# Norm, turn and split of the MLP's first chunk made inside the output projection

## What is computed

```python
x = x + attn_a(layernorm(x), Wq, bq, Wk, bk, Wv, bv, Wo, bo)   # softmax(q k^T) v, then @ Wo.T + bo
x = x + ffn(layernorm(x), gate_w, ..., down_s)                 # (silu(x @ gate) * (x @ up)) @ down
x = x + attn_b(layernorm(x), w_gate, w_up, w_down)             # silu, the smaller half set to 0, * up, @ down
x = x + ffn(layernorm(x), gate_w, ..., down_s)                 # the same weights again

def layernorm(x, eps=1e-05):
    m, v = mean(x), var(x)                                     # over the 512 features
    return (x - m) / sqrt(v + eps)
```

## Time and profile before

| | us |
|---|---|
| median of 3 runs | 1960.66 |
| lowest and highest run | 1959.5 and 1961.62 |
| the profiled execution, its own time | 1961.3 |
| span of that execution (first to last instruction) | 1959.5 |
| TensorE busy in it | 1834.5 |
| VectorE busy in it | 1426.4 |
| ScalarE busy in it | 1030.8 |
| GpSimd busy in it | 754.4 |

### The profile page before, as it was taken

How to read it: one execution, slowest core, us unless ns; L and a number is a source line. 1 busy time by engine, 2 the same in 40 slices (tenths; PEclk the granted TensorE clock), 3 DMA queues, 4 the chain that set the end, 5 groups by cost and what they waited for, 6 DMA issues and landing times.

```text
span 1959.5 us, 39587 instructions
## 1 busy us (share of the span) xinstructions
PE 1834.5 (94%) x14968; PEld 1124.2 (57%) x14968; DVE 1426.4 (73%) x2798; ACT 1030.8 (53%) x1888; POOL 754.4 (39%) x922
## 2 busy tenths in 40 slices
PE   7998888999899798998999999999999999999989
PEld 3443333333333475775776667665766766757756
DVE  6567788788882313996978888887888888878821
ACT  4334677777774122753654545635645636546411
POOL 4685656566772111224116125132142242232331
PEclk9998999899999898999999999999999999999989
DMA  7864554455433604005232213225143042161010
GB/s 245 243 196 141 146 143 123 123 144 176 137 113 122 219 1 127 12 12 151 75 126 42 91 64 104 85 62 158 41 130 88 12 152 63 33 183 54 12 41 11
DMA packets 217133, 205.70 MB, mean 105 GB/s; under 512 B 136400, under 2 KB 173264, under 8 KB 216992
## 3 DMA queue, kind: packets, MB, share of 16 engines
q1 hardware_dynamic: 210992, 187.77, 33.5%
q0 software_dynamic: 4272, 12.91, 2.0%
q10 hardware_dynamic: 1728, 3.15, 0.4%
HBM read 147.39 MB, written 33.62 MB: 92 GB/s over the span
## 4 chain that ended last, share of the span: by engine, by line
PE 55%; DVE 4%; POOL 3%; DMA 1%; issue 1%; ACT 1%; SPq 0%; DVEq 0%; ACTq 0%
PE acc L1517 14%; PE ga L1507 13%; PE ub L1507 13%; PE ga L1535 5%; PE ub L1535 5%; PE acc L1550 5%; DVE junk L1651 1%; DMA pp<-ax 1%; POOL lohi L1453 1%; POOL pp L1463 1%; POOL d_xs L1308 1%; POOL rstd_f L1271 1%; POOL ax L1469 1%; DVE kept L1701 0%; DVE junk L1686 0%
## 5 line engine op out<-in xcount | busy, mean ns | idle before, releaser
L1453 POOL TENSOR_TENSOR lohi<-h,lohi 128x256 f16<-128x256 f32 x224 | 171.8, 767 | 729.8 <-ACT lohi L1598 729.5
L1587 ACT ACTIVATE kept<-ax,T 128x1376 f16<-128x1376 f32 x248 | 356.9, 1439 | 149.7 <-DVE T L1659 146.1
L1651 DVE TENSOR_SCALAR_CACHE_REDUCE junk<-ax,T 128x1376 f16<-128x1376 f32 x248 | 405.9, 1637 | 0.9
L1067 ACT ACTIVATE pr<-s 128x512 f32<-128x512 f32 (+2 forms) x640 | 320.2, 553 | 97.5 <-PE s L956 76.9
L649 DVE TENSOR_REDUCE mx<-s 128x2 f32<-128x1024 f32 (+2 forms) x300 | 319.8, 1113 | 65.2 <-PE s L628 33.8
L1507 PE MATMUL ga<-xT_f,w_gate 128*128 128x256 f16 x2688 | 333.1, 274 | 7.2 <-DVE h L1708 3.2
L1517 PE MATMUL acc<-w_down,lohi 128*128 128x512 f16 x1344 | 327.6, 380 | 6.2 <-POOL lohi L1453 6.2
L1507 PE MATMUL ub<-xT_f,w_up 128*128 128x256 f16 x2688 | 332.6, 274 | 0.0
L1507 PEld LDWEIGHTS ga<-xT_f,w_gate 128*128 128x128 f16 x2688 | 263.8, 98 | 82.6 <-DVE h L1708 5.7
L1507 PEld LDWEIGHTS ub<-xT_f,w_up 128*128 128x128 f16 x2688 | 264.3, 98 | 31.6
L1708 DVE SCALAR_TENSOR_TENSOR h<-ub,g 128x256 f32<-128x256 f32 x224 | 93.9, 419 | 167.3 <-ACT g L1593 166.7
(11 more groups left out here) (179 smaller groups left out, 2650.7 us busy)
## 6 DMA issues: line engine op xcount, KB each, us to landing
ring<-wgu_scr SPq DMA_DIRECT2D x64, 688.0 KB, 5.3
ring<-wd_scr SPq DMA_DIRECT2D x24, 768.0 KB, 6.0
wgu_scr<-tk_h POOLq DMA_DIRECT2D x32, 172.0 KB, 2.7
q_scr<-qk_h SPq DMA_DIRECT2D x16, 256.0 KB, 2.7
k_scr<-qk_h SPq DMA_DIRECT2D x16, 256.0 KB, 4.1
v_scr<-v_f SPq DMA_DIRECT2D x16, 256.0 KB, 5.3
Q<-q_scr SPq DMA_DIRECT2D x64, 64.0 KB, 2.1
K<-k_scr SPq DMA_DIRECT2D x64, 64.0 KB, 2.1
```

The source lines that it names most:

```text
L1067: nc.scalar.activation(pr[:, g % NPR, NP * t + p0:NP * t + p1, 0:w], scores, ACT.Exp, scale=SCALE).then_inc(e2_ok, 1)
L1453: nc.gpsimd.tensor_tensor(hT[j % 2][:, 1, :], h[j % 2][:, :], hT[j % 2][:, 0, :], ALU.subtract).then_inc(hl_ok, 1)
L1587: nc.scalar.activation(kept[0][:, :], ax[k % 2][:, 1, 0:I_TK], ACT.Sign, scale=-1.0, bias=TF[:, 1:2], accum_out=cnt[:, 1:2]).then_inc(c1_o ...
L1651: nc.vector.tensor_scalar(junk[:, :], ax[k % 2][:, 0, 0:I_TK], TF[:, 0:1], -float(KZERO), ALU.is_lt, ALU.add, accum_out=cnt[:, 0:1]).then_ ...
```

## The change

What the MLP's first use does at the head of the phase is made inside the output projection's loop, on tiles 0 and 1 of X, which are complete by then. VectorE makes the statistics behind the low part of tile 4, GpSimd the root ahead of its bias addition of tile 12 (FIRST_ROOT), VectorE normalises behind the addition of tile 7 (FIRST_SCALED), TensorE turns ahead of the product of tile 9 (FIRST_TURNED), ScalarE writes the high parts behind the copy of tile 10 and VectorE the low parts behind the addition of tile 11. The result, first_xT, is a buffer that lives across the phases.

The normalised rows and ct now lie in tk_raw, so VectorE waits for tk_lo at the head of the attention's last unit. ScalarE no longer waits for the stores of x1 at the end of the phase; the semaphore x1_st lives across the phases, and in the MLP SP, GpSimd, ScalarE and VectorE wait for it at their heads (ScalarE behind its table load). TensorE doesn't. The first use has no wait of its own any more, its steps are gone from the queues, and three semaphores that each Norm had are shared, with counts one lower.

```diff
@@ build
+        first_xT = sbk("first_xT", [P, 2, KB, 2 * P], F16)
+        x1_st = keep.enter_context(nc.semaphore("x1_st"))
...
@@ phase_attend
+    FIRST_ROOT, FIRST_SCALED, FIRST_TURNED = 12, 7, 9
...
-        ct = sb("c_oT", [P, 2, 2, KB, P], F16)
+        ct = tk_raw[:, :, :].rearrange("p r n -> p (r n)")[:, 0:2 * KB * P].bitcast(F16).rearrange(
+            "p (i a k t) -> p i a k t", i=2, a=2, k=KB)
+        first_n = tk_raw[:, 2:4, :]
...
+        n_tr4 = [s2[i][:, :].rearrange("p (k t) -> p k t", k=KB) for i in range(2)]
...
@@ gpsimd
+            nc.gpsimd.memset(n_neghalf[:, :], -0.5).then_inc(n_pool, 1)
+            pool.wait_ge(n_pool, 1)
             for t in range(NTILE):
+                if t == FIRST_ROOT:
+                    pool.wait_ge(n_dve, 5)
+                    nc.gpsimd.tensor_tensor(n_rstd[:, :], n_rstd[:, :], n_neghalf[:, 0:1].broadcast_to([P, 2]), ALU.pow
+                                            ).then_inc(n_pool, 1)
                 pool.wait_ge(x_ld[t % 2], 16 * (t // 2 + 1))
...
@@ tensor
                 if t + 1 < NTILE:
                     rows(t + 1)
+                if t == FIRST_TURNED:
+                    pe.wait_ge(n_dve, 7)
+                    pe.wait_ge(e2_ok, N2 * NQ)
+                    for i in range(2):
+                        for k in range(KB):
+                            tr = nc.tensor.transpose(n_tr4[i][:, k, :], first_n[:, i, k * P:(k + 1) * P], ident[:, :])
+                        tr.then_inc(n_tr, 1)
                 for k in range(KB):
                     product(t, k)
...
@@ scalar
                 if t - 2 >= EARLY:
                     store_x(t - 2)
+                if t == FIRST_TURNED + 1:
+                    for i in range(2):
+                        act.wait_ge(n_tr, i + 1)
+                        nc.scalar.activation(first_xT[:, 0, :, i * P:(i + 1) * P], n_tr4[i], ACT.Copy).then_inc(n_hi, 1)
             store_x(NTILE - 2)
             store_x(NTILE - 1)
-            act.wait_ge(x1_st, 16 * NTILE)
...
@@ vector
+            dve.wait_ge(tk_lo, NTK)
             h = NQ // 2 - 1
             for kind, a, k in last_order():
...
             lo(EARLY)
+            for i in range(2):
+                dve.wait_ge(x_ok, i + 1)
+                nc.vector.bn_stats(n_stats[:, i, :], X[i]).then_inc(n_dve, 1)
+            dve.wait_ge(n_dve, 2)
+            for i in range(2):
+                nc.vector.bn_aggr(n_mvs[:, i, :], n_stats[:, i, :]).then_inc(n_dve, 1)
+            dve.wait_ge(n_dve, 4)
+            nc.vector.tensor_scalar(n_rstd[:, :], n_mvs[:, :, 1], EPS, XS ** -2, ALU.add, ALU.mult).then_inc(n_dve, 1)
             for t in range(EARLY, NTILE):
                 if t + 1 < NTILE:
                     lo(t + 1)
                 add(t)
+                if t == FIRST_SCALED:
+                    dve.wait_ge(n_pool, 2)
+                    for i in range(2):
+                        nc.vector.tensor_scalar(first_n[:, i, :], X[i], n_mvs[:, i, 0:1], n_rstd[:, i:i + 1],
+                                                ALU.subtract, ALU.mult).then_inc(n_dve, 1)
+                if t == FIRST_TURNED + 2:
+                    for i in range(2):
+                        dve.wait_ge(n_hi, i + 1)
+                        nc.vector.tensor_tensor(first_xT[:, 1, :, i * P:(i + 1) * P], n_tr4[i],
+                                                first_xT[:, 0, :, i * P:(i + 1) * P], ALU.subtract).then_inc(n_dve, 1)
...
@@ phase_mlp
+                self.xT = first_xT if name == first.name else sb(f"xT_{name}", [P, 2, KB, CW], F16)
...
             def ready(self, pe, u):
+                if u is first:
+                    return
...
@@ sync, gpsimd, scalar (behind preload_act_table), vector
+            sp.wait_ge(x1_st, 16 * NC * TPC)
+            pool.wait_ge(x1_st, 16 * NC * TPC)
+            act.wait_ge(x1_st, 16 * NC * TPC)
+            dve.wait_ge(x1_st, 16 * NC * TPC)
...
-            norms["f1"].on_pool(pool, first)
-            norms["f1"].on_tensor(pe, first)
-            norms["f1"].on_scalar(act, first)
-            statistics(first)
-            norms["f1"].normalise(dve, first)
-            norms["f1"].low_parts(dve, first)
...
             def take_in(s, t):
+                if s.use is first:
+                    dve.wait_ge(x_in[0], 16)
```

More of the change, by code:

```diff
@@ L120, in build @@
             phase_attend(nc, ident, sc, o_scr, pieces, FIRST_PIECES, dq, wgT, wuT, wdT, wgu_scr, wd_scr,
-                         x, WoT, bo, x1_scr)
-        phase_mlp(nc, ident, w_gate, w_up, w_down, wgu_scr, wd_scr, x1_scr, out)
+                         x, WoT, bo, x1_scr, x1_st, first_xT)
+        phase_mlp(nc, ident, w_gate, w_up, w_down, wgu_scr, wd_scr, x1_scr, x1_st, first_xT, out)
 def quantised_pieces(quantised):
@@ L715, in phase_attend @@
         o_in = sb("o_in", [P, 2, D], F32)
-        ct = sb("c_oT", [P, 2, 2, KB, P], F16)
+        ct = tk_raw[:, :, :].rearrange("p r n -> p (r n)")[:, 0:2 * KB * P].bitcast(F16).rearrange(
+            "p (i a k t) -> p i a k t", i=2, a=2, k=KB)
+        first_n = tk_raw[:, 2:4, :]
+        n_stats = sb("n_stats", [P, 2, 6], F32)
+        n_mvs = sb("n_mvs", [P, 2, 2], F32)
+        n_rstd = sb("n_rstd", [P, 2], F32)
+        n_neghalf = sb("n_neghalf", [P, 1], F32)
+        n_tr4 = [s2[i][:, :].rearrange("p (k t) -> p k t", k=KB) for i in range(2)]
         X = [t[:, r, :] for t in (dq_f, dq_z[:, :, :].bitcast(F32), dq_s) for r in range(NDB)]
@@ L747, in phase_attend @@
         x_ok = sem("cx_ok")
-        x1_st = sem("x1_st")
+        n_pool = sem("n_pool")
+        n_dve = sem("n_dve")
+        n_tr = sem("n_tr")
+        n_hi = sem("n_hi")
         NDQ = len(pieces)
@@ L1187, in attend_order, with phase_mlp @@
     return order
-def phase_mlp(nc, ident, w_gate, w_up, w_down, wgu_scr, wd_scr, x1_scr, out):
+def phase_mlp(nc, ident, w_gate, w_up, w_down, wgu_scr, wd_scr, x1_scr, x1_st, first_xT, out):
     TPC = 2
@@ L1250, in tile_of @@
             return X[:, c % XR, t, :]
+        stages = mlp_stages(NC, GU, DU, TPC, RING, DG, XR)
+        first = stages[0].use
         class Norm:
             def __init__(self, name):
-                self.xT = sb(f"xT_{name}", [P, 2, KB, CW], F16)
+                self.xT = first_xT if name == first.name else sb(f"xT_{name}", [P, 2, KB, CW], F16)
                 self.stats = sb(f"stats_{name}", [P, TPC, 6], F32)
@@ L1324, in on_tensor @@
                         m = nc.tensor.transpose(tr[t][:, k, :], xn[:, t, k * P:(k + 1) * P], ident[:, :])
-                    m.then_inc(self.tr_ok, 1)
+                    m.then_inc(d_tr_ok, 1)
             def on_scalar(self, act, u):
                 for t in range(TPC):
-                    act.wait_ge(self.tr_ok, TPC * u.aparts + t + 1)
+                    act.wait_ge(d_tr_ok, TPC * u.aparts + t + 1)
                     nc.scalar.activation(self.xT[:, 0, :, t * P:(t + 1) * P], tr[t][:, :, :], ACT.Copy
-                                         ).then_inc(self.hi_ok, 1)
+                                         ).then_inc(d_hi_ok, 1)
             def ready(self, pe, u):
+                if u is first:
+                    return
                 if u.apart:
-                    pe.wait_ge(self.lo_ok, TPC * (u.aparts + 1))
+                    pe.wait_ge(d_lo_ok, TPC * (u.aparts + 1))
                 else:
@@ L1339, in phase_mlp @@
         norms = {"f1": Norm("f1"), "g": Norm("g"), "f2": Norm("f2")}
+        d_tr_ok = sem("d_tr_ok")
+        d_hi_ok = sem("d_hi_ok")
+        d_lo_ok = sem("d_lo_ok")
         xh_ok = sem("d_xh_ok")
@@ L1371, in phase_mlp @@
         o_st = sem("o_st")
-        stages = mlp_stages(NC, GU, DU, TPC, RING, DG, XR)
-        first = stages[0].use
         def ring_count(s, gates, downs):
@@ L1855, in mlp_stages @@
     uses = {"f1": [], "g": [], "f2": []}
-    aparts = {"f1": 0, "g": 0, "f2": 0}
-    shifts = 0
+    aparts, shifts = -1, 0
     for p, s in enumerate(stages):
@@ L1866, in mlp_stages @@
             name = "f2" if name == "f1" else "f1"
-        s.use = Use(name, s.c, len(uses[name]), None if source is None else stages[at[source]],
-                    uses[name][-1] if uses[name] else None, apart, aparts[name], shifts)
+        s.use = Use(name, s.c, len(uses[name]) - (name == "f1"), None if source is None else stages[at[source]],
+                    uses[name][-1] if uses[name] else None, apart, aparts, shifts)
         uses[name].append(s)
         if apart:
-            aparts[name] += 1
+            aparts += 1
             if p:
```

10 lines of the change are left out of this document (4 added, 6 removed).

## The result

| | before | after |
|---|---|---|
| median of the first four runs of each | 1961.14 | 1937.33 |
| lowest and highest of them | 1959.5, 1966.24 | 1936.32, 1940.17 |
| ratio after / before, 95% interval | | 0.9899 [0.9876, 0.9923] |
| the profiled execution, its own time | 1961.3 | 1940.17 |
| its span, and the mean granted clock | 1959.5, 0.977 | 1938.4, 0.985 |

The account below looks back on a forecast made before the run. TensorE, busy 94% of the span, was taken as the bound, with 15.2 us between the projection's last and the MLP's first product. Moving the third block from 689.49 to 674.14 took 15.35 us off 1960.66: 1945.3 us, range 1943.0 to 1949.0.

Parts of the forecast that it names:

- The chain of the seam and the earlier barrier: Between projection and MLP: 11.94 us of load, norm, transposes and split go; the barrier no longer waits for the last store.
- rival 2: At the barrier: an engine's exit still lasts until the store has landed; 11.9 us less, 1948.8 us; chance 0.07.
- some 2.7 us behind the last product: Sign that the forecast is right: the MLP's first gate product starts this long after the projection's last product.
- Eight transposes: On TensorE in the projection, between tiles 8 and 9: they cost 0.87 us, with bounds of 0 and 1.98.
- VectorE's added work at no cost: In the projection: statistics, two normalisations and two low parts cost nothing; without cover they would cost 4.4 us.
- rival 3: In the projection: normalisations are held up while GpSimd works, 2.32 us each, costing 2.06 us, giving 1947.4; chance 0.05.
- GpSimd's root: Ahead of tile 12's bias addition in the projection: 0.72 us, later additions end by 643.9 instead of 643.14, no cost.
- The constants: GpSimd's memsets at the MLP's head, behind the moved wait: h is made by 673.0, 1.1 us before TensorE asks.
- The wait on the weight split: New wait on tk_lo heading VectorE's last attention unit: GpSimd's last split ended long before at 571.57, so no cost.
- rival 4: VectorE's wait on tk_lo delays its division; slower than before from 606.4; chance 0.04, shared with whatever else undoes the gain.
- rival 1: At the seam: the clock falls over the 1.8 us gap, so 13.7 us less, giving 1947.0; chance 0.27.
- The sum: The MLP's third block moves from 689.49 to 674.14, everything behind it as a whole: 15.35 us less, 1945.3 us.

Follow-up runs that it names:

- warm_fill: The changed kernel with 16 unread matmuls ahead of the transposes at two later places where a norm has no cover; 1938.75 us, ratio to before 0.9896.
- after_again: The changed kernel run again, unchanged; median 1943.08 us, ratio 0.9929 to the kernel before beside it.
- before_again: The kernel before run again, unchanged; median of 12 runs 1957.77 us, ratio 1.0009 to the other runs of before.
- wait_only: The kernel before with only the wait for the x1 stores moved into the MLP, the norm staying at its head; 1954.13 us, ratio 0.999.
- seam_fill: The kernel before with 30 unread matmuls in TensorE's queue at the MLP's head, ahead of the eight transposes; 1953.46 us, ratio 0.9985.
- norm_only: The changed kernel with ScalarE's wait for the stores put back at the end of the projection phase; 1945.4 us, ratio 0.9941 to before.

## Why the prediction was right in its terms and wrong in its time

- *The chain of the seam and the earlier barrier:* right. The first gate product was put 668.03 - 666.25 = 1.78 us behind the last product, and came 1.55 or 1.56 behind it in all traces of the changed kernel. The 0.22 us are in TensorE's start: 667.14 against ScalarE's 667.10, so 0.04 us where the other seam showed 0.29. The barrier didn't wait for the stores (rival 2): ScalarE's drain took 0.16 us. The sign "some 2.7 us behind the last product" doesn't follow from the prediction's own sum: it is 668.90 - 666.25, with the transposes counted into the start of the gate product and not into the end of the last product.
- *Eight transposes:* right, 645.11 - 644.23 = 0.88 us against 0.87.
- *VectorE's added work at no cost:* right; tiles still follow each other every 648.13 - 645.11 = 3.02 us.
- *The normalisations* (rival 3): the hold is there, but smaller than the rival had it, and covered. In after they took 0.54 us each, while GpSimd waited for a load. In six other traces one of GpSimd's additions (1.25 to 1.54 us) ran beside them and one of the two took longer: 0.94 us in warm_fill, 1.49 to 1.60 in the others. In each of the six, tile 9's product still followed the transposes at once. In after_again (ns min/median/max of the two; then GpSimd):

```profile
L1208 DVE TENSOR_SCALAR tk_raw<-dq_w_a,n_mvs,n_rstd x2: 537/1016/1495, 639.2 to 639.6; 128x512 f32<-128x512 f32 x2
```

```profile
639.32 2.92 POOL L949 TENSOR_TENSOR pr<-pr,bo_all 128x512 f32<-128x512 f32 x2 [3.73 <-DMA pr<-in_x]
```

So the hold was at most 1.60 - 0.54 = 1.06 us, no longer than one addition. The Trainium skill ("SBUF — State Buffer", "SBUF: two separate sides") has one of the two engines keep the ports that they share for a whole instruction, and these traces agree. The 2317 ns of the earlier trace rows, beside a string of short memsets, came again in before_again, wait_only and seam_fill (2316 to 2318) and stay longer than one instruction's hold; no run here takes that string apart.
- *GpSimd's root:* the cost of nothing was right, the step was not. The last bias addition was put at 643.9 at the latest and ended at 645.97 + 1.27 = 647.24. The loads behind the root were issued later and then took longer to come (2.06 us of waiting ahead of the last). The tile that needs that addition, 15, is added at 665.62, so 18.4 us of cover hid the delay. The argument against rival 3, that GpSimd has nothing left after 643.9, falls with it.
- *The constants:* right. h of the first block was ready at 671.41, 0.97 us ahead of the third block, with 1.1 forecast; the constants were what it waited for.
- *The wait on the weight split* (rival 4): no cost, right. The last split ended at 572.29 + 1.16 = 573.45, and VectorE's division started at 592.39. That is past the 591 named as a sign, but TensorE's product released it, not the split.
- *The clock at the seam* (rival 1 against the forecast): the forecast was right. The gap of 1.55 to 1.56 us kept the higher level in all seven traces that have it; norm_only's 3.24 us lost it, at 1.56 us where 1.69 were put. The reason given, that eight of nine such gaps in one trace kept it, was too strong: of the gaps of 1.5 to 1.9 us in the attention 21 of 26 lost it, so length alone doesn't decide. That the gap came out 0.22 us shorter than put was luck, and whether 1.78 us would have kept the clock here no run shows.
- *The sum:* the third block was put 674.14 - 667.12 = 7.02 us behind the last product; it came at 6.8. The difference of 15.35 us compares with 23.24 - 6.80 - 0.88 = 15.6 in the traces and 15.4 [13.3, 17.5] between the means of 20 and 67 runs.
- *The step that failed* is the one from the difference to the time: "the median is 1960.66; from the median I get 1945.3", with the runs of before taken to "lie 2.1 us apart". Three runs had been taken for the kernel's own time. Single runs of it lie 18 us apart, and their mean is 1956.8; from there the same difference gives 1941.4, which is the mean of the changed kernel's 20 runs, and below the range. The miss of 1945.3 - 1937.33 = 8.0 us is thus 3.9 us of a base that lay high and 4.1 us of four runs that lay low; as far as the 20 and 67 runs show, the size of the change has no part in it. Below the forecast the range had 2.3 us, for transposes that cost nothing and a few falls of the clock in the MLP. The falls in the attention, ahead of the change, had no term at all, and there the traces of the changed kernel differ by 11.5 us. With 4 us for the base and 4 us for the new runs the range would have reached down to 1937.

What stays open: why a gap of the same length costs the clock in one execution and not in another. Nor is it settled why the first four runs of each kernel lay on opposite sides. Their means differ by 24.2 us. By the scatter (4.3 us for one run, so 2.2 for a mean of four and 3.0 for the difference of two such means) that is nearly three errors from 15.4, more than chance readily gives. The two chips of the experiments both gave the smaller difference; the chip of the first runs isn't known, so that it gives more of its own stays possible.

## What to carry to other kernels

A step at the head of a phase that waits for data from the far side of a barrier is worth moving when the producing phase has idle time on every engine it needs; its price is then only what the bound engine itself issues (0.9 us here against 16.4). Moving the wait and moving the work belong together: alone the wait gave at most 0.5 us, behind the moved work 3.25. And before a time is forecast to 0.2%, look at how far single runs lie apart and at the granted clock of the trace: a difference can be right to 0.3 us while the time it is taken from is off by 4.

## What was not expected of the hardware

TensorE has 22 to 28 gaps of 1 to 5.3 us in a run here, of which 6 to 13 were followed by the lower level, and the clock makes most of the scatter: 18.4 us between the fastest and the slowest of 67 runs of one program, at a correlation of -0.91 with the mean granted clock. Gaps of equal length fared differently by place: of those of 1.5 to 1.9 us, 21 of 26 in the attention lost the clock and none of seven at the seam. Matmuls that nobody reads, 30 of them in an idle stretch, brought 2.8 us back in the two blocks that followed. And TensorE's first matmul behind a barrier came 0.04 us after ScalarE's first instruction, where it had come 0.29 us after it at the other seam.
